# Attention's scalings on ScalarE, two row additions beside other stages, and each gather's first counts fetched one stage ahead

## The chip, the cores and the metric

The kernel runs on one core of a Trainium2 chip, in a single launch. The metric is the device time of one execution in microseconds (us). A core has a matrix engine (TensorE, in the rows PE; PEld is its loading of weights), a vector engine (VectorE, DVE), an activation engine (ScalarE, ACT), a general-purpose engine (GpSimd, POOL), and a queue that here only issues transfers (SyncE, SP). Each works through its own list of instructions in order; semaphores tie them together.

## The reference

Four layers, each a graph step and a feed-forward step, over 2500 nodes of 256 features and 80000 edges. Every step normalises x over its features, computes something and adds it to x:

```python
edge_index = jnp.stack([src, dst])
x = x + L0_gnn(layernorm(x))     # (mean over a node's edges) @ W_l.T + x @ W_r.T + b_r
x = x + L0_ffn(layernorm(x))     # two picked experts (gelu), then layer_norm(...) * gamma + beta
x = x + L1_gnn(layernorm(x))     # normalised sum over edges, @ W.T + b, layer norm, relu
x = x + L1_ffn(layernorm(x))     # 6 routed experts, 2 per node
x = x + L2_gnn(layernorm(x))     # gelu(agg @ W1 + b1) @ W2 + b2
x = x + L2_ffn(layernorm(x))     # 8 routed experts, 2 per node
x = x + L3_gnn(layernorm(x))     # attention of 4 heads over the edges, elu(out + b)
x = x + L3_ffn(layernorm(x))     # 8 experts, all weighted
```

In the attention, per head: e = exp(leaky_relu(el[src] + er[dst])), rowsum = segment_sum(e, src), and the output of a node is the sum over its edges of e / max(rowsum, 1e-12) times a row of x @ W, then elu(out + b).

## The kernel before

**Data.** The nodes are padded to 2560, 20 tiles of 128 (NT), 5 blocks of 512 (NB), 4 tiles to a block (TB). x stays in SBUF all the time as `m.x` (a tile's 128 nodes on the partitions, 256 features each). `m.xT` holds features on the partitions; `m.xn` and `m.o` are tiles of the size of x that the stages use in turn. The edges are turned once into a dense matrix of edge counts between nodes, in 16-bit floats, kept in device memory (`m.A_high`, transposed `m.AT_high`, and a low part that is only needed for large counts). A sum over edges is then a matrix product with the counts.

**Stages.** `program` (L2453) runs a list of phases. Each is a block with one list of instructions per engine; a new phase begins when all engines have ended the one before. In order, with the start in the profiled execution where the text needs it: setup and counts with a degree stage (`prepare`, L252, 360 us), gather g0 (380 us), experts e0 (526 us), norm n2 (664 us), norm n3 (696 us), gather g1 (709 us), routed experts e1, norm n6 (1085 us), gather g2 (1099 us), experts e2 (1200 us), the row addition b2 (1325 us), norm n8 (1334 us), routed experts e3 (1362 us), n9, attention (its main loop from 1716 to 2067 us), n10 (2068 us), experts e4 (2087 us to the end).

**A gather** (`phase_gather`, L772) multiplies the counts with y, 5 blocks of 512 result columns one after another. y is split into a high part (ScalarE, L936) and a low part (VectorE, L954), in 5 chunks of 4 tiles; TensorE waits for chunk after chunk in its first block. For each block TensorE runs 80 products of a 128 x 128 piece of y with 512 columns of counts (L877, the last two L895). A block's counts are 2,560 KB, in one of two buffers `at`. SP loads the first block's in five pieces when the phase begins (L835), each with its own semaphore, and every further block in one piece (L843), from the third on only when the block two before is through. Gather g0 writes its normalised rows to `m.o`, g1 to `m.xn`; both write `m.xT` behind a block's product, as g2 does.

**A norm** (`phase_norm`, L655): VectorE takes statistics of 20 tiles (L696), seven small steps on 20 columns (L241 to L247), a copy (L700), ScalarE the root, VectorE the reciprocal, then the rows are scaled, by ScalarE where there is a gamma (L745). n2 finishes layer 0's experts: gamma times the row, plus beta, plus x. There GpSimd adds beta to x by itself, block by block (L735), once both rows are loaded (L683, L684), while VectorE takes statistics of another tile; VectorE then multiplies by gamma (L718), waits for the block's beta (`shifted`) and adds to x (L721). n6 precedes g2 and n3 precedes g1.

**The experts** (`phase_experts`, L1580): TensorE computes a block's hidden values (`layer0`, L1743) one block ahead of the second product (`last`, L1771). ScalarE applies gelu twice (L1861, L1862), VectorE takes the low part (L2024) and adds results to the destination (L2047). Weights are split likewise: high part by ScalarE (L1868), low part by GpSimd (L1688, `low_weights`), which otherwise has nothing to do in this phase. In e0 the destination is `m.o` and x isn't touched; in e2 it is x.

**b2** (`phase_add_row`, L2065) loads one row to all partitions and adds it to all of x on VectorE.

**The attention loop** (`phase_attention`, L2082): 10 iterations, 2 pairs of heads times 5 blocks. In each, VectorE makes 40 masked count tiles (`mask`, L2318), ScalarE 20 plain ones (L2398), and TensorE multiplies them with the weighted features (L2426), masked ones for two heads (u = 1, 2) and plain ones for both (u = 0). ScalarE evicts each sum from PSUM (`evict`, L2386). The finishing of an iteration runs one iteration later in VectorE's list, as single steps put between pairs of masks by a generator:

```python
if (u - 1) * NT + t >= 8 and t % 2:
    next(steps, None)
```

Its steps: add two halves (L2329), scale by a factor per node and head (`s_g`, L2331), subtract and add four others (L2333 to L2339), four small ones for 1/rowsum (L2342 to L2348), scale by it (L2350), add the bias (L2354); then ScalarE takes an exponential (`exps`, L2390), and VectorE adds to x in two steps (L2360, L2362). In ScalarE's list `evict(it - 1, 2)` comes after five plain tiles of an iteration, and `evict(it, 0)`, `exps(it - 1)` and `evict(it, 1)` after its twenty.

## Time and profile before

| | |
|---|---|
| runs | 2480.57, 2481.78, 2483.63 us; median 2481.78 |
| profiled execution | 2481.93 us, its span 2480.2 us |
| busy share of the span | TensorE 78%, VectorE 61%, ScalarE 46%, GpSimd 15% |
| mean granted clock of TensorE | 0.89 of full speed |
| transfers | 222.59 MB, 90 GB/s on average |

The times are of the whole kernel; the shares are averages over stages that have different limits, so a change in one stage is read from that stage. The granted clock has two levels here, 1.00 (2.4 GHz) and 0.50 (1.2 GHz); values between are means over a stretch. In the rows, a tile's name leaves out its number (`g_at` is the gather's `at`), and two instructions of one engine may overlap by some 0.1 us, so what an instruction costs in a series is the time from one start to the next.

### The profile page before, as it was taken

The page shows a single profiled execution, that of the slowest core. Times are in us where ns is not written, and L with a number is a line of the kernel's source. Part 1 is how long each engine was busy: PE and PEld are TensorE (multiplying, and loading weights), DVE is VectorE, ACT ScalarE, POOL GpSimd, SP SyncE. Part 2 cuts the span into 40 slices and gives each one's busy share as a digit, 9 for nine tenths or more (in the row PEclk, how much of TensorE's full clock was granted, in tenths as well). Part 3 has the DMA queues.
Part 4 walks back from the last instruction along what each step waited for, and adds up shares of the span by engine and source line. Part 5 has one row for each costly group of instructions (what it writes and reads, how often), then busy time and mean ns, then how long its engine had stood idle before and what let it go on. Part 6 is the DMA issues. An engine that isn't in the chain of part 4 may idle for free. (4 is left out here: it accounts for less than half of the span.)

```text
span 2480.2 us, 38997 instructions
## 1 busy us (share of the span) xinstructions
PE 1941.6 (78%) x12631; PEld 1564.9 (63%) x12632; DVE 1519.1 (61%) x2808; ACT 1130.5 (46%) x2105; POOL 367.5 (15%) x319
## 2 busy tenths in 40 slices
PE   4888888949649659829795499644999995999997
PEld 2455554539625348704594499624988884788886
DVE  7997772454555356650335555377999995555554
ACT  0468882125221148610443277423443442566674
POOL 1000000000100037700000477422000000001010
PEclk9999999969869869959897599866999996899999
DMA  1235554210033136543101355321333220000001
GB/s 52 95 139 210 209 208 153 78 35 1 5 124 113 36 109 194 154 167 128 35 1 49 124 168 170 109 75 52 96 103 101 75 73 28 2 26 13 26 13 42
DMA packets 135056, 222.59 MB, mean 90 GB/s; under 512 B 18237, under 2 KB 100669, under 8 KB 134771
## 3 DMA queue, kind: packets, MB, share of 16 engines
q1 hardware_dynamic: 124775, 192.62, 23.0%
q0 software_dynamic: 10128, 27.93, 3.6%
q8 instruction: 96, 1.57, 0.3%
q14 instruction: 57, 0.47, 0.1%
HBM read 146.26 MB, written 74.24 MB: 89 GB/s over the span
## 5 line engine op out<-in xcount | busy, mean ns | idle before, releaser
L877 PE MATMUL g_ps<-g_at,g_y 128*128 128x512 f16 x1170 | 261.7, 384 | 125.5 <-DMA g_at<-counts_t_high 119.9
L2024 DVE TENSOR_TENSOR e_h_low<-x_feat,e_h_high 128x512 fp32r<-128x512 f32 (+1 forms) x240 | 169.5, 709 | 233.7 <-ACT e_h_high L1862 233.7
L877 PEld LDWEIGHTS g_ps<-g_at,g_y 128*128 128x128 f16 x1170 | 115.3, 99 | 266.6 <-DMA g_at<-counts_t_high 121.1
L2318 DVE SCALAR_TENSOR_TENSOR att_masked<-dinv_row,att_thr,x_feat 128x512 fp32r<-128x512 f32 x400 | 276.8, 747 | 9.2 <-PEq L2150 3.0
L1861 ACT ACTIVATE x_feat<-e_hps,e_b 128x512 f32<-128x512 f32 (+1 forms) x240 | 177.7, 741 | 209.8 <-issue 99.6
L2426 PE MATMUL att_ps<-att_xl_parts,att_masked 128*128 128x260 f32 x1600 | 244.3, 291 | 22.3 <-DVE att_masked L2318 20.9
L2426 PEld LDWEIGHTS att_ps<-att_xl_parts,att_masked 128*128 128x128 f32 x1600 | 211.0, 189 | 40.6 <-DVE att_masked L2318 32.4
L478 DVE TENSOR_TENSOR hot_key<-o_tok,dinv_row x240 | 195.7, 816 | 0.0
L526 PE MATMUL count_ps<-hot_key,hot_lo 128*128 x960 | 178.6, 311 | 18.4 <-DVE hot_key L478 14.5
L1771 PE MATMUL e_yps<-e_w_high,e_h_high 128*128 128x256 f32 (+1 forms) x640 | 183.0, 286 | 2.2 <-DVE e_h_low L2024 2.2
L1771 PE MATMUL e_yps<-e_w_high,e_h_low 128*128 128x256 f32 (+1 forms) x640 | 181.7, 284 | 0.0
L1771 PE MATMUL e_yps<-e_w_low,e_h_high 128*128 128x256 f32 (+1 forms) x640 | 181.6, 284 | 0.0
L1862 ACT ACTIVATE e_h_high<-e_hps,e_b 128x512 fp32r<-128x512 f32 (+1 forms) x240 | 176.6, 736 | 0.0
L2398 ACT ACTIVATE att_plain<-x_feat 128x512 fp32r<-128x512 f16 x200 | 117.8, 627 | 78.4 <-PE att_ps L2426 73.8
L2426 PE MATMUL att_ps<-att_xl_parts,att_plain 128*128 128x260 f32 x800 | 125.4, 288 | 30.0 <-ACT att_plain L2398 30.0
L526 PEld LDWEIGHTS count_ps<-hot_key,hot_lo 128*128 x960 | 95.1, 99 | 80.2 <-issue 42.7
L1743 PE MATMUL e_hps<-e_x_high,e_w_high 128*128 128x512 f32 (+1 forms) x320 | 126.7, 396 | 21.1 <-POOL e_w_low L1688 20.0
L1413 POOL DMA_INDIRECT e_x_rows<-xn_rows,e_get_i x104 | 126.5, 1216 | 59.1 <-issue 29.6
L581 ACT ACTIVATE turn_high<-count_ps 128x320 f16<-128x320 f32 x160 | 74.6, 466 | 119.6 <-PE count_ps L534 90.3
L478 DVE TENSOR_TENSOR hot_lo<-o_tok,dinv_row 128x512 f16 x240 | 100.3, 418 | 46.0 <-PE count_ps L526 38.4
L2426 PEld LDWEIGHTS att_ps<-att_xl_parts,att_plain 128*128 128x128 f32 x800 | 109.3, 192 | 30.1 <-ACT att_plain L2398 30.1
L1688 POOL TENSOR_TENSOR e_w_low<-a3xn_tok,e_w_high 128x512 fp32r<-128x512 f32 x23 | 29.1, 1295 | 660.6 <-ACT e_w_high L1868 660.6
(481 smaller groups left out, 4725.5 us busy)
## 6 DMA issues: line engine op xcount, KB each, us to landing
g_at<-counts_t_high SPq DMA_DIRECT2D x12, 2560.0 KB
x_feat<-counts_high SPq DMA_DIRECT2D x40, 640.0 KB, 4.1
e_w_in<-in_L_ffn_W SPq DMA_DIRECT2D x35, 512.0 KB, 3.8
e_w_in<-in_L_ffn_expert_w SPq DMA_DIRECT2D x56, 256.0 KB, 3.8
counts_t_high<-turn_high SPq DMA_DIRECT2D x20, 640.0 KB, 4.6
counts_t_low<-turn_low SPq DMA_DIRECT2D x20, 640.0 KB, 5.9
counts_high<-count_row SPq DMA_DIRECT2D x20, 640.0 KB, 2.9
counts_low<-count_row SPq DMA_DIRECT2D x20, 640.0 KB, 4.1
```

The costliest lines, as they stand in the source:

```text
L478: return dve.tensor_tensor(out.rearrange("p u (w d) -> p u w d", d=2), numbers.rearrange("p (w d) -> p w d", d=2).unsqueeze(1).to_broadcas ...
L526: mm = pe.matmul(acc[:, q % 4, 0:KW], hot_lo[:, j, ds(slot, P)], hot_key[:, j, ds(slot, KW)], start=False, stop=False, skip_group_check=True)
L877: pe.matmul(ps[:, k, :], y2[:, part, s, k * P:(k + 1) * P], at[:, b % 2, :, s, :], start=(s == 0 and part == 0), stop=False, skip_group_ch ...
L1413: pool.indirect_dma_start(x_rows[:, b % XB, q, :], None, m.xn_rows[:, :], bass.IndirectOffsetOnAxis(ap=r.get_i[:, b * RT + q:b * RT + q + ...
L1743: mm = pe.matmul(h_ps[0][:, f, 0:width(b)], w_parts[0][w][:, u, k, f * P:(f + 1) * P], x_parts[x][:, k, b * BLK:b * BLK + width(b)], start ...
L1771: mm = pe.matmul(y_ps[0:tokens, q, 0:D], h_parts[-1][h][:, v % 2, k, q * P:q * P + tokens], w_parts[-1][w][:, u, k, :], start=(k == 0 and ...
L1861: act.activation(h_sb[i][:, f, 0:w], h_ps[i][:, f, 0:w], func, bias=bias, scale=scale)
L1862: act.activation(h_parts[i][0][:, v % 2, f, 0:w], h_ps[i][:, f, 0:w], func, bias=bias, scale=scale).then_inc(h_act[i], 1)
L2024: dve.tensor_tensor(h_parts[i][1][:, v % 2, f, 0:w], h_sb[i][:, f, 0:w], h_parts[i][0][:, v % 2, f, 0:w].bitcast(F32), ALU.subtract).then_ ...
L2318: dve.scalar_tensor_tensor(S[:, n % RING, :], EL[:, it % 2, u - 1, :], thr[:, t, h:h + 1], A[:, t, :], ALU.is_gt, ALU.mult).then_inc(maske ...
L2398: act.activation(plain[:, n % ARING, :], A[:, t, :], ACT.Copy).then_inc(plain_a, 1)
L2426: mm = pe.matmul(ps[:, n % 2 * TB + q, 0:PW], side[:, q * P:(q + 1) * P], moving, start=(t == 0), stop=(t == NT - 1))
```

## The change

- Attention: the two wide scalings leave VectorE. The scaling by `s_g` is done by ScalarE in the eviction of u = 1 and 2: instead of one instruction over four tiles, four of 130 columns with a scale pointer and one for the other columns of all four. The scaling by 1/rowsum becomes eight instructions of 64 columns ahead of the exponential in `exps`. VectorE signals that 1/rowsum is made, leaves one step empty, and waits for the eight before it adds the bias.
- `phase_add_row` is gone. Its row is loaded at the start of g2 (ahead of the counts) and added to x by GpSimd, block by block, in g2.
- Beta leaves n2. Its row is loaded in e0 behind the first weights and added to x by GpSimd in e0, block by block, behind the low weights of the second expert.
- A gather's first block of counts gets a place of its own and is loaded in an earlier stage, as one transfer of 2,560 KB: for g0 in `prepare`, into `m.o`, when the counts are stored; for g1 in n2 and for g2 in n6, into `m.xT`. SP waits for it at that stage's end. The five pieces and their semaphores go, and the third block is loaded without waiting, because the first no longer uses a buffer of `at`.

```diff
 prepare, sync
             sp.sem_inc(written, 1)
+            tile, src = ahead
+            sp.dma_start(tile, src).then_inc(ahead_in, 16)
             sp.wait_ge(kept, 1)
...
             sp.wait_ge(stored, 16)
+            sp.wait_ge(ahead_in, 16)
 phase_norm, sync
+            if ahead is not None:
+                for tile, src in ahead:
+                    sp.dma_start(tile, src).then_inc(ahead_in, 16)
+                sp.wait_ge(ahead_in, 16 * len(ahead))
 phase_norm, vector
-                    if shift_x:
-                        dve.wait_ge(shifted, b + 1)
+                    if finish == "add":
                         dve.tensor_tensor(xv, v, xv, ALU.add).then_inc(ready, TB)
 phase_norm, gpsimd
-            if shift_x:
-                pool.wait_ge(affine_in, 32)
-                for b in range(NB):
-                    xv = part(m.x, b)
-                    pool.tensor_tensor(xv, xv, gb[:, 1:2, :].to_broadcast([P, TB, D]), ALU.add).then_inc(shifted, 1)
 phase_gather, sync
-            for c in range(NB):
-                cut = slice(c * TB, (c + 1) * TB)
-                sp.dma_start(at[:, 0, :, cut, :], m.AT_high[0:TB, :, c * BLK:(c + 1) * BLK].rearrange(
-                    "t p (s n) -> p t s n", n=P)).then_inc(first_in[c], 16)
+            if row is not None:
+                sp.dma_start(bias_sb[:, :], row.partition_broadcast(P)).then_inc(bias_in, 16)
...
-                if b >= 2:
+                if b >= 3:
                     sp.wait_ge(agg_mm, b - 1)
 phase_gather, tensor
+            def columns(b, s):
+                return at[:, b % 2, :, s, :] if b else first[:, :, s, :]
...
-                        pe.wait_ge(first_in[s // TB], 16)
                         pe.wait_ge(y_low, s // TB + 1)
 phase_gather, gpsimd
+            if row is not None:
+                pool.wait_ge(bias_in, 16)
+                for b in range(NB):
+                    xv = part(m.x, b)
+                    pool.tensor_tensor(xv, xv, bias_sb[:, :].unsqueeze(1).to_broadcast([P, TB, D]), ALU.add)
 phase_experts, sync
             load_pair(sp, 0)
+            if row is not None:
+                sp.dma_start(row_sb[:, :], row.partition_broadcast(P)).then_inc(row_in, 16)
 phase_experts, gpsimd
             low_weights(pool, 0, 1, 0)
+            if row is not None:
+                pool.wait_ge(row_in, 16)
+                for b in range(NB):
+                    xv = m.x[:, b * TB:(b + 1) * TB, :]
+                    pool.tensor_tensor(xv, xv, row_sb[:, :].unsqueeze(1).to_broadcast([P, TB, D]), ALU.add)
 phase_attention, finish (vector)
-                    own.join(dve.tensor_tensor(ov, ov, sg.unsqueeze(3).to_broadcast([P, TB, GRP, DA]), ALU.mult))
-                    yield
...
-                    own.join(dve.tensor_tensor(rs[:, 1, :, :], rs[:, 1, :, :], sf, ALU.mult))
+                    dve.tensor_tensor(rs[:, 1, :, :], rs[:, 1, :, :], sf, ALU.mult).then_inc(rs_made, 1)
                     yield
-                    own.join(dve.tensor_tensor(fin[:, :, :, :], o[:, :, :, 0:DO],
-                                               rs[:, 1, :, :].unsqueeze(3).to_broadcast([P, TB, GRP, DO]), ALU.mult))
                     yield
+                    dve.wait_ge(fin_scaled, (it + 1) * TB * GRP)
 phase_attention, evict and exps (scalar)
+                    for q in range(TB):
+                        t = it % NB * TB + q
+                        act.activation(sums[:, it % 2, q, u, 0:2 * DA], banks[:, q, 0:2 * DA], ACT.Copy,
+                                       scale=s_g[:, t, h:h + 1])
+                    act.activation(sums[:, it % 2, :, u, 2 * DA:PW], banks[:, :, 2 * DA:PW], ACT.Copy).then_inc(evicted, 1)
...
                 def exps(it):
+                    act.wait_ge(rs_made, it + 1)
+                    for q in range(TB):
+                        for u in range(GRP):
+                            act.activation(fin[:, q, u, :], o[:, q, u, 0:DO], ACT.Copy,
+                                           scale=rs[:, 1, q, u:u + 1]).then_inc(fin_scaled, 1)
                     act.wait_ge(fin_done, it + 1)
 program
+        first0 = first_view(m.o[:, :, :].rearrange("p t d -> p (t d)"))
+        first = first_view(m.xT[:, :, :].rearrange("p k n -> p (k n)"))
...
-            lambda: phase_add_row(nc, m, "b2", i["L2_gnn_b2"]),
```

## Rows read from the trace of the kernel before

**Rows 1.** Table by stretch, attention: start:end, length, busy time (count) per engine, clock, DMA.

```profile
1780.00:1812.00 32.00, 29.43 (x225) 27.57 (x224) 31.43 (x51) 15.05 (x24) 0.00 (x0) 1.00 0.28 85
```

**Rows 2.** Who waited for whom, attention loop: total us, times, longest.

```profile
ACT att_neg L2390 <- DVE att_fin L2354: 78.3, 9, 9.1
```

**Rows 3.** Order of time, VectorE in attention's second iteration: start, duration, instruction, count.

```profile
1751.01 0.69 DVE L2329 TENSOR_TENSOR att_o<-att_acc 128x520 f32<-128x520 f32 x1
1751.73 1.41 DVE L2318 SCALAR_TENSOR_TENSOR att_masked<-dinv_row,att_thr,x_feat 128x512 fp32r<-128x512 f32 x2
1753.06 0.69 DVE L2331 TENSOR_TENSOR att_o<-att_o,att_s_g 128x520 f32<-128x520 f32 x1
...
1768.09 0.16 DVE L2348 TENSOR_TENSOR att_rs<-att_rs,att_s_f 128x8 f32<-128x8 f32 x1
...
1769.62 0.68 DVE L2350 TENSOR_TENSOR att_fin<-att_o,att_rs 128x512 f32<-128x512 f32 x1
```

**Rows 4.** Order of time, norm n2.

```profile
667.26 11.53 POOL L735 TENSOR_TENSOR x_tok<-x_tok,n_gb 128x1024 f32<-128x1024 f32 x5 [85.82 <-DMA n_gb<-in_L_ffn_gamma]
670.47 1.47 DVE L241 TENSOR_TENSOR n_mean<-n_st 128x20 f32<-128x20 f32 x1
...
679.22 0.18 DVE L700 COPY n_var<-n_var 128x20 f32<-128x20 f32 x1
...
680.21 9.94 ACT L745 ACTIVATE o_tok<-o_tok,n_off,n_tmp 128x256 f32<-128x256 f32 x20 [0.56 <-DVE n_off L706]
```

**Rows 5.** Order of time, norm n3.

```profile
702.20 0.19 DVE L241 TENSOR_TENSOR n_mean<-n_st 128x20 f32<-128x20 f32 x1
...
703.21 0.18 DVE L700 COPY n_var<-n_var 128x20 f32<-128x20 f32 x1
```

**Rows 6.** Order of time, the starts of the gathers g0, g1 and g2.

```profile
381.33 5.77 DVE L954 SCALAR_TENSOR_TENSOR g_y<-xn_tok,g_y 128x1024 f16<-128x1024 f32 x5 [4.95 <-ACT g_y L936]
...
386.91 15.46 PE L877 MATMUL g_ps<-g_at,g_y 128*128 128x512 f16 x64 [10.64 <-DMA g_at<-counts_t_high]
...
710.29 5.77 DVE L954 SCALAR_TENSOR_TENSOR g_y<-xn_tok,g_y 128x1024 f16<-128x1024 f32 x5 [2.03 <-ACT g_y L936]
...
716.76 19.09 PE L877 MATMUL g_ps<-g_at,g_y 128*128 128x512 f16 x78 [54.39 <-DMA g_at<-counts_t_high]
...
1100.32 5.76 DVE L954 SCALAR_TENSOR_TENSOR g_y<-e1xn_tok,g_y 128x1024 f16<-128x1024 f32 x5 [2.03 <-ACT g_y L936]
...
1103.01 18.83 PE L877 MATMUL g_ps<-g_at,g_y 128*128 128x512 f16 x78 [54.82 <-DMA g_at<-counts_t_high]
```

**Rows 7.** Order of time, b2 and the start of n8.

```profile
1325.57 0.34 SPq L2072 DMA_DIRECT2D b_row<-in_L_gnn_b  x1
...
1334.62 0.34 SPq L683 DMA_DIRECT2D n_gb<-in_L_ffn_beta  x1
```

**Rows 8.** Table by stretch, the first five us of g1's first block.

```profile
716.00:721.00 5.00, 4.24 (x10) 1.49 (x11) 0.05 (x1) 0.00 (x0) 0.00 (x0) 0.50 1.09 387
```

**Rows 9.** Order of time, experts e0, VectorE and GpSimd.

```profile
570.71 0.69 DVE L2024 TENSOR_TENSOR e_h_low<-x_feat,e_h_high 128x512 fp32r<-128x512 f32 x1 [2.25 <-ACT e_h_high L1862]
...
576.68 4.76 POOL L1688 TENSOR_TENSOR e_w_low<-xn_tok,e_w_high 128x1024 fp32r<-128x1024 f32 x2 [28.17 <-ACT e_w_high L1868]
...
581.93 0.69 DVE L2024 TENSOR_TENSOR e_h_low<-x_feat,e_h_high 128x512 fp32r<-128x512 f32 x1 [2.25 <-ACT e_h_high L1862]
```

**Rows 10.** Waits of SP's queue, degree stage.

```profile
SPq L293 <- DMA counts_low<-count_row: 1.7, 1, 1.7
```

**Rows 11.** Order of time, degree stage, GpSimd.

```profile
370.08 1.20 POOL L314 DMA_INDIRECT spare_low<-counts_low,spare_at_i  x1 [8.91 <-DVE spare_at_i L400]
```

**Rows 12.** Order of time, ScalarE in attention's second and third iterations.

```profile
1764.92 1.04 ACT L2386 ACTIVATE att_acc<-att_ps 128x1040 f32<-128x1040 f32 x1 [3.17 <-PE att_ps L2426]
...
1781.96 3.22 ACT L2398 ACTIVATE att_plain<-x_feat 128x512 fp32r<-128x512 f16 x6
```

**Rows 13.** Order of time, ScalarE in e4, bias and scale by pointer.

```profile
2199.59 0.78 ACT L1861 ACTIVATE x_feat<-e_hps,e_b 128x512 f32<-128x512 f32 x1
```

More of the change, by code:

```diff
@@ L651, in phase_counts, with phase_norm @@
         all_stored += [(row_stored[u], NT // 2 * 32) for u in range(2)]
-        prepare(nc, m, mats, all_stored)
-def phase_norm(nc, m, name, src, out, outT=None, gamma=None, beta=None, scale=None, finish=None, kept=None, twice=False):
+        prepare(nc, m, mats, all_stored, m.first_block(m.o))
+def phase_norm(nc, m, name, src, out, outT=None, gamma=None, beta=None, scale=None, finish=None, kept=None, twice=False,
+               ahead=None):
     sem = nc.alloc_semaphore
@@ L712, in _ @@
             if gamma is not None:
-                dve.wait_ge(affine_in, 32)
+                dve.wait_ge(affine_in, 16 if beta is None else 32)
                 ga, be = (gb[:, i:i + 1, :].to_broadcast([P, TB, D]) for i in range(2))
@@ L767, in _, with phase_gather @@
                         mm.then_inc(turned, 1)
-def phase_gather(nc, m, name, y, kind, w=None, w_self=None, bias=None, gamma=None, beta=None, kept=None):
+def phase_gather(nc, m, name, y, kind, first, row=None, w=None, w_self=None, bias=None, gamma=None, beta=None, kept=None):
     sem = nc.alloc_semaphore
     at_in = [sem(f"{name}_at_in{i}") for i in range(2)]
-    first_in = [sem(f"{name}_first_in{c}") for c in range(NB)]
     agg_mm, agg_out, lin_mm, lin_out, bias_in, selfed, y_high, y_low, low_in, low_used = (
@@ L1648, in phase_experts @@
             wT = m.o[:, :, :].rearrange("p t d -> p (t d)")[0:EX, 0:NP].rearrange("p (t n) -> p t n", t=NT)
+        row_sb, row_in = sb("row", [P, D]) if row is not None else None, sem(f"{name}_row_in")
         def width(b):
@@ L2062, in _ @@
             pair(pairs - 1, False)
-def phase_add_row(nc, m, name, row):
-    sem = nc.alloc_semaphore
-    row_in = sem(f"{name}_in")
-    with nc.sbuf_tensor(f"{name}_row", [P, D], F32) as r, nc.Block() as block:
-        @block.sync
-        def _(sp):
-            sp.dma_start(r[:, :], row.partition_broadcast(P)).then_inc(row_in, 16)
-        @block.vector
-        def _(dve):
-            dve.wait_ge(row_in, 16)
-            dve.tensor_tensor(m.x[:, :, :], m.x[:, :, :], r[:, :].unsqueeze(1).to_broadcast([P, NT, D]), ALU.add)
 def phase_attention(nc, m, W, Wl, Wr, b):
```

48 lines of the change are left out of this document (30 added, 18 removed).

## The prediction

> **What bounds the kernel now.** I read the chain of waits first. It only shows the last stage, whose matmuls follow one another and which the change leaves alone, so I went stage by stage through the stretches that the change touches: a table by stretch, the list of who waited for whom, and the order of time. Four different limits came out.
>
> In the attention loop it is VectorE. In a stretch of 32 us, about one iteration, it is busy for 31.43 us, TensorE for 29.43 and ScalarE for 15.05 [rows 1]; ScalarE stands idle for 78.3 us over nine iterations at the exponential, waiting for VectorE [rows 2]. A mask pair takes 1.33 us of VectorE and each of the wide finishing steps between the pairs 0.72 (2.05 from one to the next) [rows 3].
>
> In the norm n2 it is a wait that no semaphore explains. Seven tiny statistics steps take from 670.47 to 679.22, 8.75 us [rows 4]; in n3 the same ones take from 702.20 to 703.21, 1.01 us [rows 5]. The only difference in that stretch is GpSimd adding beta: five adds in 11.53 us, 2.31 each, and one VectorE instruction gets through per add [rows 4].
>
> At the start of the three gathers it is a transfer. The first low parts of y are ready 1.22 us after L954's start, at 382.55, 711.51 and 1101.54 (5.77 us for five, so some 1.15 from one to the next), but the first matmul starts at 386.91, 716.76 and 1103.01 and waits for the counts [rows 6].
>
> Between e2 and n8 it is a stage of its own: b2's row load is issued at 1325.57 and n8's first load at 1334.62 [rows 7].
>
> **The change part by part.**
>
> *b2 goes.* Its whole stage is on the path: 1334.62 - 1325.57 = **9.05 us**. Its work, five adds on GpSimd, goes into g2. The row's load is ahead of g2's large loads in SP's queue, a small transfer. GpSimd starts when the row has landed. VectorE's L954 reads two SBUF tiles there, so it may alternate with the adds, as the tiny steps did in n2; each later low part could then be up to 2.31 us late. TensorE needs a new part only every 16 matmuls (ten in 4.24 us at the clock of a gather's start [rows 8], so some 6.8; at twice that clock 3.4, about the 2.31 + 1.15 of an add and a low part). I take nothing; the bounds are nothing and one add, 2.3 us, since a gain is excluded by the first part being made before.
>
> *n2 without beta on GpSimd.* The statistics should take what they take in n3: 8.75 - 1.01 = **7.74 us**. Behind them ScalarE's 20 scalings (9.94 us) and VectorE's adds stay as they are [rows 4]. The beta load leaves n2's queue, so gamma comes sooner; neither is waited for.
>
> *Beta beside e0.* GpSimd's queue has the adds behind its low weights of the second expert, which end at 576.68 + 4.76 = 581.44, and VectorE's first low part after that starts at 581.93; one round of the stage is 11.22 us (570.71 to 581.93) [rows 9]. The adds would run to some 593. By the n2 rows they may delay each of a round's four low parts (0.69 us each) by one add of 2.31: 4 x 2.31 = 9.2 us of delay in a round of which VectorE fills a third. The consumer, the second product, comes about one round later, and a block's hidden values are double-buffered. I take **nothing**, with 0 to 11.5 us (five adds, TensorE idle for all of it) as bounds. The row's load is queued behind the weights.
>
> The Trainium skill (SBUF — State Buffer, section "SBUF: two separate sides") speaks against this move: it says that GpSimd and a VectorE instruction with two SBUF inputs share a port pair that one of them holds for its whole instruction, while the other stands. This trace agrees, with 2.31 us per step in n2 [rows 4]; by that rule alone, without a round of slack, the sum would lose 11.5 us here.
>
> *The counts fetched one stage ahead.* For each gather 2,560 KB; at 387 GB/s, the rate of such loads at g1's start, that is 6.6 us [rows 8]. In n2 and n6 next to nothing else moves and both stages outlast it. SP waits for it at the end of the stage, so the cover is the rest of the stage; if that were gone, 6.6 us each. In the degree stage it is issued when the count stores have landed, after a wait of 1.7 us by SP [rows 10], some us before GpSimd's row fetch goes out at 370.08 [rows 11]. The end of that stage hangs on this fetch. I take nothing, with 0 to 6.6 us. SP's own store of the spare row waits behind the issue only, a fraction of a us. In the gathers the second and third blocks are then loaded at once, well ahead of use.
>
> Each gather's first matmul then follows the first low part: 386.91 - 382.55 = 4.36, 716.76 - 711.51 = 5.25, 1103.01 - 1101.54 = 1.47, minus 0.06 each for the hand-over: **10.9 us** [rows 6]. TensorE's clock is 0.50 (1.2 GHz) from 716 to 721, the first 5 us of work after idling through n2 and n3 [rows 8]. It starts as cold after the change, so this slow stretch moves along with the start. Whether it is shorter or longer is not to be read here: at most half of 5 us either way for a start.
>
> *Attention: what leaves VectorE.* L2331 and L2350, 0.72 us each, in nine iterations: 9 x 1.44 = **13.0 us**. TensorE doesn't take over: its 240 matmuls of an iteration need at most 240/225 x 29.43 = 31.4 us, VectorE's shortened iteration some 33 (20 pairs of 1.33, eight wide steps of 0.72, four small ones of 0.20) [rows 1, 3].
>
> *What ScalarE gets.* No row has a Copy with a scale pointer of this size, so I build it. A plain 512-element copy: 0.63 us, from one to the next (3.22 - 0.63)/5 = 0.52; the 1040-element eviction 1.04, so 0.78 ns an element and 0.12 us of fixed spacing; the activation with two pointers 0.78 instead of 0.63, so 0.075 a pointer [rows 12, 13]. A scaled one of 64 is then 0.12 + 0.05 + 0.075 = 0.245 us, eight with the last one's tail 2.07. An eviction becomes four of 130 (0.295 each) and one of 520: 1.82 instead of 1.04. The upper end is the dearest scaled row, 256 elements with two pointers, 9.94/20 = 0.50 us each [rows 4]; I take the low value, since cost follows the elements in the rows that I have.
>
> *The wait that this adds.* VectorE has two mask pairs between giving out the reciprocals and asking for the scaled rows. Counted from its first finishing step (1751.01), the reciprocals are out at 5 x 2.05 + 3 x 1.53 + 0.2 = 15.0 and asked for at 17.7: 2.7 us for 2.07 and 0.1 of hand-over [rows 3]. It fits. ScalarE arrives at this place in its queue behind the eviction at 1764.92 + 1.04, which is 14.95 after that step; with the longer eviction 15.7, so VectorE would wait 0.1 us there [rows 3, 12]. In most other iterations ScalarE has more in hand: it idled 8.7 us on average, 9.1 at most [rows 2]. Queued behind a longer wait would be all of VectorE's masks and through them TensorE. The longer eviction at an iteration's start delays TensorE by 0.78 us, within its slack.
>
> *The tail.* After the last mask nothing hides anything: eviction +0.78, L2331 -0.73, L2350 -0.73 and 2.17 for the scalings: +1.5 us. Attention: 13.0 - 1.5 - 0.1 = **11.4 us**.
>
> **Sum.** 9.05 + 7.74 + 10.9 + 11.4 = 39.1 us off the profiled execution's 2481.93 (span 2480.2): 2442.8. That execution is 0.15 us above the median of the runs, so **2442.7 us**.
>
> **Rivals.**
>
> *GpSimd's adds hold up e0.* For it: the n2 rows. Against: the round of slack. Five adds of 2.31 us: 2442.7 + 11.5 = 2454 us. Chance 0.08, for so far the trace shows the stall and not a case where it is hidden. This is what the port rule of the Trainium skill (SBUF — State Buffer, the same section) comes to if nothing takes up the delay.
>
> *Scalings too dear for two mask pairs.* At 0.50 us each, eight take 4.0; VectorE waits 1.4 us in each of nine iterations (12.5), and the tail is 2.7 longer: 2442.7 + 12.5 + 2.7 = 2458 us. For it: small instructions have a floor that I only extrapolate. Against: the two-pointer row costs just 0.15 more than the plain one. Chance 0.10.
>
> *The same mechanism on the other side, slower than before.* It decides when the wait per iteration eats 39.1/9 = 4.3 us: eight scalings in 2.7 + 4.3 - 0.1 = 6.9, 0.86 us each. At 0.9 us: 4.6 us in each of nine iterations and 5 in the tail, 2442.7 + 46 = 2489 us. Against it, the dearest scaled row is 0.50 us at four times the elements. Chance 0.03.
>
> *The early fetch lengthens the degree stage.* The spare row's fetch stands behind 2,560 KB: 6.6 us, 2449 us. For it: both go through the same DMA engines. Against: different queues, and the large one starts some us earlier. Chance 0.06.
>
> *The fetch doesn't do what it says:* the first matmul waits for something else, and the starts stay: 2442.7 + 10.9 = 2454 us. Against: both inputs of that matmul have a row [rows 6]. Chance 0.04.
>
> **The numbers.** My forecast has 0.69. The range reaches up to 2456, over both cases at 2454 and the one at 2449, and leaves out the two dear-scaling cases (0.13). Down it goes to 2438: attention's full 13.0 (1.6 more), and some 3 us from shorter slow stretches at the starts. 0.2%, 5 us, is about what a measurement of this kernel can tell from no change; every case but one is faster by more: 0.95, and 0.02 for the middle, 0.03 for slower.
>
> **What would show it.** In n2, the step from L241 to the copy before the root at about 1 us. No b2 stage. In each gather, the first matmul right behind the first low part. In attention, iterations some 1.4 us shorter, and next to no VectorE idle time released by ScalarE before the bias add. In e0, VectorE low parts of up to 3 us beside GpSimd's adds, and no TensorE idle time behind them. Wrong: VectorE waiting over 0.5 us an iteration for scaled rows; TensorE idle in e0 around 590; the degree stage ending later than 22 us after its start.

## The result, and the profile after

The changed kernel takes 2441.94 us (median of 4 runs, 2441.44 to 2442.75), the kernel before 2481.65 beside it (4 runs, 2480.57 to 2483.63): a ratio of 0.9837 with a 95% interval of 0.9821 to 0.9852 (the two medians alone give 0.9840). The prediction was 2442.7 in a range of 2438 to 2456. The profiled execution of the changed kernel took 2441.66 us, its span is 2440.0, 40.2 less than before. One of all the executions below, of experiment 7's kernel, took 5025.92 us at a mean granted clock of 1.00, for a reason that is not known, and is left out.

Where the 40.2 us come from is read from the transfers: in both kernels each stage but n3, n6, n9 and n10 begins with one that SP issues. The lengths from one such start to the next, in one profiled execution of each kernel:

| stage | before, us | after, us | difference | predicted |
|---|---|---|---|---|
| setup and counts | 360.07 | 360.27 | +0.20 | 0 |
| degree stage | 20.14 | 21.16 | +1.02 | 0 |
| g0 | 145.81 | 141.92 | -3.89 | -4.30 |
| e0 | 137.73 | 137.67 | -0.06 | 0 |
| n2 and n3 | 45.42 | 37.73 | -7.69 | -7.74 |
| g1 | 147.35 | 142.04 | -5.31 | -5.19 |
| e1 and n6 | 242.69 | 243.67 | +0.98 | 0 |
| g2 | 100.52 | 99.23 | -1.29 | -1.41 |
| e2 | 125.84 | 125.93 | +0.09 | 0 |
| b2 | 9.05 | gone | -9.05 | -9.05 |
| n8 | 27.53 | 27.18 | -0.35 | 0 |
| e3 and n9 | 284.93 | 284.39 | -0.54 | 0 |
| attention and n10 | 439.66 | 426.25 | -13.41 | -11.4 |
| e4 | 393.46 | 392.56 | -0.90 | 0 |

The four places named in the prediction give 9.05 + 7.69 + 10.49 + 13.41 = 40.6; the rest is the degree stage and stages whose work the change leaves alone (in n8 the two row loads change places).

**Norm n2**, VectorE in order of time in the changed kernel (start, duration, instruction, count). It answers to [rows 4]: the small steps take 1.02 us from L241 to the copy, as in n3 [rows 5].

```profile
667.74 0.19 DVE L241 TENSOR_TENSOR n_mean<-n_st 128x20 f32<-128x20 f32 x1
...
668.76 0.18 DVE L709 COPY n_var<-n_var 128x20 f32<-128x20 f32 x1
```

**The gathers' starts**, the same view, for g0, g1 and g2. They answer to [rows 6].

```profile
382.54 5.76 DVE L961 SCALAR_TENSOR_TENSOR g_y<-xn_tok,g_y 128x1024 f16<-128x1024 f32 x5 [4.98 <-ACT g_y L943]
...
383.82 17.41 PE L876 MATMUL g_ps<-o_tok,g_y 128*128 128x512 f16 x71 [6.37 <-DVE g_y L961]
...
699.86 5.77 DVE L961 SCALAR_TENSOR_TENSOR g_y<-xn_tok,g_y 128x1024 f16<-128x1024 f32 x5 [2.02 <-ACT g_y L943]
...
701.14 18.98 PE L876 MATMUL g_ps<-x_feat,g_y 128*128 128x512 f16 x78 [41.51 <-DVE g_y L961]
...
1085.58 12.23 DVE L961 SCALAR_TENSOR_TENSOR g_y<-e1xn_tok,g_y 128x1024 f16<-128x1024 f32 x5 [2.02 <-ACT g_y L943]
...
1086.86 18.98 PE L876 MATMUL g_ps<-x_feat,g_y 128*128 128x512 f16 x78 [53.22 <-DVE g_y L961]
1087.40 14.94 POOL L921 TENSOR_TENSOR x_tok<-x_tok,g_bias 128x1024 f32<-128x1024 f32 x5 [49.63 <-DMA g_bias<-in_L_gnn_b]
```

Each first product now waits for the low part (the name after the arrow) and starts 1.28 us after VectorE began it, where it waited for the counts before. In g2 GpSimd's additions stretch the five low parts from 5.76 to 12.23 us, and TensorE goes through its 78 products in 18.98 us all the same (18.83 before [rows 6], and 18.98 in g1, which has no additions).

**Experts e0**: first GpSimd's and VectorE's instructions in order of time, then a table by stretch (start:end, length, busy time (count) of PE, PEld, DVE, ACT and POOL, granted clock, DMA share, GB/s).

```profile
578.67 13.63 POOL L1739 TENSOR_TENSOR x_tok<-x_tok,e_row 128x1024 f32<-128x1024 f32 x5
...
579.19 10.85 DVE L2040 TENSOR_TENSOR e_h_low<-x_feat,e_h_high 128x512 fp32r<-128x512 f32 x4 [2.25 <-ACT e_h_high L1878]
589.96 1.65 DVE L2063 SCALAR_TENSOR_TENSOR o_tok<-e_yps,pair_w,o_tok 128x256 f32<-128x256 f32 x4
```

```profile
581.30:587.30 6.00, 6.00 (x50) 5.92 (x49) 6.00 (x4) 1.80 (x3) 6.00 (x3) 1.00 0.00 0
587.30:593.30 6.00, 6.00 (x35) 5.55 (x35) 6.00 (x8) 4.17 (x8) 5.00 (x2) 1.00 0.01 3
```

Four low parts of 0.69 us take 10.85, 2.7 each, the length of one addition (13.63 / 5); the last ends 6.1 us later after the stage's start than before (66.7 us for 60.6). TensorE is busy for 6.00 of 6.00 us beside it, and the stage is as long as before. So the stall that the Trainium skill (SBUF — State Buffer, section "SBUF: two separate sides") describes is there in full, and nothing on the path waits for it.

**The attention**: the table by stretch for one iteration, VectorE's and ScalarE's own waits (total us, times, longest), and both engines in order of time. The two SP rows are the same point of two iterations, seven apart.

```profile
1773.00:1806.00 33.00, 31.21 (x242) 29.51 (x241) 32.53 (x53) 18.28 (x40) 0.00 (x0) 1.00 0.31 97
```

```profile
ACT att_fin L2398 <- DVE att_rs L2346: 23.5, 9, 4.7
...
DVE att_fin L2351 <- ACT att_fin L2398: 2.1, 1, 2.1
```

```profile
1740.04 0.16 DVE L2346 TENSOR_TENSOR att_rs<-att_rs,att_s_f 128x8 f32<-128x8 f32 x1
1740.11 2.73 DVE L2318 SCALAR_TENSOR_TENSOR att_masked<-dinv_row,att_thr,x_feat 128x512 fp32r<-128x512 f32 x4
1742.77 0.68 DVE L2351 TENSOR_TENSOR att_fin<-att_fin,att_bias 128x512 f32<-128x512 f32 x1
...
1740.45 2.01 ACT L2398 ACTIVATE att_fin<-att_o,att_rs 128x64 f32<-128x64 f32 x8
...
1744.02 1.13 ACT L2390 ACTIVATE att_acc<-att_ps,att_s_g 128x130 f32<-128x130 f32 x4
1745.03 0.62 ACT L2392 ACTIVATE att_acc<-att_ps 128x520 f32<-128x520 f32 x1
...
1739.48 12.44 SPq L2146 DMA_DIRECT2D x_feat<-counts_high  x4
...
1970.95 12.44 SPq L2146 DMA_DIRECT2D x_feat<-counts_high  x4
```

In the kernel before, the mask behind the last small step ([rows 3] have the step, at 1768.09), and the same point of two iterations:

```profile
1768.28 1.42 DVE L2318 SCALAR_TENSOR_TENSOR att_masked<-dinv_row,att_thr,x_feat 128x512 fp32r<-128x512 f32 x2
```

```profile
1765.97 13.53 SPq L2146 DMA_DIRECT2D x_feat<-counts_high  x4
...
2008.49 13.52 SPq L2146 DMA_DIRECT2D x_feat<-counts_high  x4
```

An iteration takes (1970.95 - 1739.48) / 7 = 33.07 us, and took (2008.49 - 1765.97) / 7 = 34.65 before. VectorE is still the limit (32.53 busy of 33.00, TensorE 31.21), and it waits for scaled rows once, in the tail.

**The degree stage**, the stretch from 370 to 374, first in the kernel before, then in the changed one:

```profile
370.00:374.00 4.00, 3.55 (x13) 1.47 (x12) 3.11 (x15) 2.73 (x5) 1.20 (x1) 1.00 0.41 164
```

```profile
370.00:374.00 4.00, 3.66 (x10) 1.75 (x8) 2.12 (x11) 2.01 (x4) 1.15 (x1) 0.58 1.01 422
```

The early fetch moves 422 GB/s here, but what is slower is TensorE, whose granted clock is 0.58 on average instead of 1.00; its ten products for the degree row take 6.28 us instead of 5.21, and the stage's last steps hang on them.

### The profile page after: what moved, and what is told of

It reads as the page before. It is cut to its first block and busy times, and to the rows that moved or that the text cites. A ratio compares the mean times of both kernels' runs of the same rounds, so it can differ in the third digit from the quotient of the medians.

```text
span 2440.0 us, 39066 instructions
## 1 busy us (share of the span) xinstructions
PE 1935.5 (79%) x12631; PEld 1562.2 (64%) x12632; DVE 1506.2 (62%) x2787; ACT 1162.7 (48%) x2265; POOL 385.5 (16%) x324
## 5 line engine op out<-in xcount | busy, mean ns | idle before, releaser
L2040 DVE TENSOR_TENSOR e_h_low<-x_feat,e_h_high 128x512 fp32r<-128x512 f32 (+1 forms) x240 | 178.0, 746 | 228.6 <-ACT e_h_high L1878 228.6
L2437 PE MATMUL att_ps<-att_xl_parts,att_masked 128*128 128x260 f32 x1600 | 236.0, 288 | 15.1 <-DVE att_masked L2318 11.4
L876 PE MATMUL g_ps<-g_at,g_y 128*128 128x512 f16 x936 | 205.3, 379 | 5.6 <-DVE x_feat L999 5.6
L876 PEld LDWEIGHTS g_ps<-g_at,g_y 128*128 128x128 f16 x936 | 91.3, 98 | 114.4 <-issue 7.5
```

The lines of the kernel that those rows point to most:

```text
L876: pe.matmul(ps[:, k, :], y2[:, part, s, k * P:(k + 1) * P], columns(b, s), start=(s == 0 and part == 0), stop=False, skip_group_check=True)
L2040: dve.tensor_tensor(h_parts[i][1][:, v % 2, f, 0:w], h_sb[i][:, f, 0:w], h_parts[i][0][:, v % 2, f, 0:w].bitcast(F32), ALU.subtract).then_ ...
L2437: mm = pe.matmul(ps[:, n % 2 * TB + q, 0:PW], side[:, q * P:(q + 1) * P], moving, start=(t == 0), stop=(t == NT - 1))
```

## The experiments

All start from the changed kernel. They were measured later than the comparison above; beside them the kernel before took 2483.11 to 2485.15 us (medians), the changed kernel 2444.02 and 2445.82, ratios of 0.9838 and 0.9842. So times are compared by their ratio to the kernel before, and stage by stage. Stages that no experiment touches wander from execution to execution: e1 with n6 between 242.7 and 246.2 us, e3 with n9 between 284.3 and 286.3, e4 between 392.6 and 394.7. So do, where their work is the changed kernel's, g2 (98.9 to 100.0), e2 (124.3 to 126.2) and the attention with n10 (426.3 to 427.8).

### 1. The scalings on VectorE again

`phase_attention` of the kernel before, the rest as changed:

```diff
+own.join(dve.tensor_tensor(ov, ov, sg.unsqueeze(3)..., ALU.mult))
+own.join(dve.tensor_tensor(fin, o[..., 0:DO], rs[:, 1, :, :].unsqueeze(3)..., ALU.mult))
-act.activation(fin[:, q, u, :], o[:, q, u, 0:DO], ACT.Copy, scale=rs[:, 1, q, u:u + 1])
```

> Only the attention is as before: both scalings on VectorE, everything else as changed. Theory: the iteration goes from 33.07 us back to 34.64, nine times 1.57, and the tail gets 1.2 shorter, so 2441.9 + 14.1 - 1.2 = 2454.9 us. Of the 1.57, 1.44 are the two wide steps and 0.12 is VectorE's wait for its own last small step, which is not there when that step signals ScalarE instead. Rival: part of the attention's gain comes from elsewhere (an earlier start of the loop, another clock of TensorE); then the iteration stays under 34.4 us and the time under 2453. The degree stage and e1, each 1.0 us longer than before in the profile of the changed kernel, should be as long here as there if the change is the reason, and may be anything within 1 us if they wander from execution to execution.

Measured: 2458.27 us, ratio 0.9904 (0.9887 to 0.9920), 0.0067 or some 16 us above the changed kernel's; its attention with n10 took 440.05 us, 13.8 more than in the changed kernel, 0.4 more than before, and an iteration 34.65. All of the attention's gain sits in these steps. The whole kernel's 16 us are 3 more than the 13.0 expected, with some 4 us of uncertainty; two of its four executions took 2455.7 us and two 2461, and the profiled one is of the faster two. The degree stage took 20.62 us here and e1 245.36: both wander.

### 2. The first counts loaded in the gather, and 3. the rows behind them

First, SP issues five pieces into the same place when the gather begins; then, in the second kernel, the gather's small rows come behind the pieces in SP's queue instead of ahead of them:

```diff
+for c in range(NB):
+    sp.dma_start(first[:, :, cut, :], m.AT_high[0:TB, :, c * BLK:(c + 1) * BLK]...).then_inc(first_in[c], 16)
...
+pe.wait_ge(first_in[s // TB], 16)
 pe.wait_ge(y_low, s // TB + 1)
```

> Each gather loads its first counts itself again, in five pieces when it begins, into the place where the changed kernel keeps them. Theory: the first matmul starts 4.4, 5.2 and 1.5 us after the first low part again, and the three gathers get 3.9 + 5.3 + 1.3 = 10.5 us longer: 2452.4 us. If the early fetch is what made the degree stage 1.0 us longer (21.16 instead of 20.14), that comes back: 2451.4; if it is where TensorE's granted clock happened to rise and fall, the stage is not bound to be 20.1. Rival: the gathers' starts hang on the low parts of y alone, and the fetch ahead gains next to nothing: under 2445 us.

> The gathers load their first counts themselves again, as in the run with the fetch in the gather, but the rows (bias, gamma and beta, and in g2 the row that GpSimd adds) are queued behind the five pieces instead of ahead of them. In the kernel before, the first piece was there 3.8 us after its issue in g2, where no row was ahead of it, and 6.3 us in g0 and g1, where one and three were; in the run with the fetch in the gather, where g2 has a row ahead, 5.7. Theory: a row that is spread to all partitions holds back the transfer behind it by some 2 us; then the first matmul starts 3.8 us after the first issue in all three gathers, which gives back 2.1 + 1.0 + 1.9 of that run's 2456 (in g1 the issue of the rows' 1.3 us as well): 2449 to 2452 us. Rival: the 2 us belong to where the transfer comes from or to what ran before, and the first matmuls still start 5.7 to 6.3 us after the first issue: 2455 us.

Measured: 2456.22 us, ratio 0.9890 (0.9873 to 0.9906), with the rows ahead; 2447.63, ratio 0.9851 (0.9831 to 0.9871), with the rows behind. The start of g2 in the first and in the second, in order of time:

```profile
1093.02 4.56 SPq L834 DMA_DIRECT2D x_feat<-counts_t_high  x5
...
1098.75 19.05 PE L879 MATMUL g_ps<-x_feat,g_y 128*128 128x512 f16 x78 [57.10 <-DMA x_feat<-counts_t_high]
```

```profile
1085.33 2.73 SPq L827 DMA_DIRECT2D x_feat<-counts_t_high  x5
...
1089.25 18.54 PE L879 MATMUL g_ps<-x_feat,g_y 128*128 128x512 f16 x78 [54.92 <-DMA x_feat<-counts_t_high]
```

From the first issue to the first product it is 5.73 us with a row ahead and 3.92 without; 5.60 and 3.88 in g0, 6.30 and 4.19 in g1. With the row ahead SP also takes longer to issue the five pieces (4.56 us for 2.73). So the starts do hang on the counts, and a large part of that wait was the small rows ahead of them. The gathers of the first kernel are 3.44, 5.86 and 3.84 us longer than in the changed one, 13.1 in all where 10.5 was expected: g2 now has a row ahead of its pieces, which it had not before. The second kernel's are 2.36, 1.82 and 1.10 longer, 5.3 in all, and its 2447.63 us fits the 2447.2 that this gives; swapping the rows gave back 7.9 us, the sign and the place that the theory named and more than its 5.0 to 6.3. In these two kernels, without a fetch in it, the degree stage took 20.16 us.

### 4. Beta in n2 again

```diff
+pool.tensor_tensor(xv, xv, gb[:, 1:2, :].to_broadcast([P, TB, D]), ALU.add).then_inc(shifted, 1)
...
+dve.wait_ge(shifted, b + 1)
```

> Beta is added by GpSimd in n2 again, and not in e0. Theory: n2's small steps from L241 to the copy go from 1.02 us back to about 8.8, so 2441.9 + 7.7 = 2449.6 us, and e0 stays at 137.7 us, since its adds cost nothing. Rival: the adds cost something in e0 that its unchanged length hides; then e0 gets shorter here by that much, and the time lies below 2448. Second rival: n2's stall was the load of beta, which fetched gamma later, and not the adds; then VectorE is not held for 2.3 us per step beside them.

Measured: 2450.25 us, ratio 0.9867 (0.9850 to 0.9883); n2 with n3 took 47.16 us, 9.4 more than in the changed kernel, and e0 137.68. GpSimd and VectorE in n2, in order of time:

```profile
665.49 11.54 POOL L744 TENSOR_TENSOR x_tok<-x_tok,n_gb 128x1024 f32<-128x1024 f32 x5 [87.69 <-DMA n_gb<-in_L_ffn_beta]
666.84 1.04 DVE L241 TENSOR_TENSOR n_mean<-n_st 128x20 f32<-128x20 f32 x1
667.80 2.37 DVE L242 TENSOR_TENSOR n_tmp<-n_st 128x20 f32<-128x20 f32 x1
...
674.66 0.16 DVE L245 TENSOR_SCALAR n_var<-n_var 128x20 f32<-128x20 f32 x1
...
677.31 0.18 DVE L709 COPY n_var<-n_var 128x20 f32<-128x20 f32 x1
```

VectorE's steps of 0.2 us end where GpSimd's additions end (2.31 us each from 665.49), and the last of them run when the five are through at 677.03: the adds are the stall, and e0 is no shorter without them. Not only steps with two inputs in SBUF are held: L244, with one, ran for 2.25 us (0.18 in n3), while the statistics of 256 columns ahead of L241, with one too, took their 0.41 us beside an addition. The size was off, because n2 is held until the additions end, and they began 5.37 us after the stage here and 3.51 before: beta's row, now the second and with the 2,560 KB queued right behind it, was there 4.97 us after its issue (at 660.52), where the second row of before took 3.10.

### 5 and 6. ScalarE's scalings cut into two, and into four

```diff
-act.activation(fin[:, q, u, :], o[:, q, u, 0:DO], ACT.Copy, scale=...)
+for w in range(0, DO, DO // 2):    # DO // 4 in the second kernel
+    act.activation(fin[:, q, u, w:w + DO // 2], o[:, q, u, w:w + DO // 2], ACT.Copy, scale=...)
```

> Each of ScalarE's eight scalings of 1/rowsum is cut into two of 32 columns; the result is the same. VectorE asks for the scaled rows 2.73 us after it began the last of its small steps, and in the changed kernel they are there after 2.2, so 0.5 us of room is left. Theory (a fixed part of 0.12 + 0.075 us per instruction and 0.78 ns an element, as in the prediction): sixteen take 3.5 us, VectorE waits 1.0 us in each of nine iterations and the tail grows by 1.5: 2441.9 + 9 + 1.5 = 2452.4 us. Rival: a floor per instruction as high as what the 64 columns took (0.25): 3.95 us, 1.45 us of waiting, 2441.9 + 13 + 2 = 2457 us. Second rival: cost follows the elements, or other engines have room for the wait: 2442 us.

> Each scaling of 1/rowsum is cut into four of 16 columns, 32 instructions in all; the result is the same. With the fixed part that two sizes now show (2.02 us for eight of 64 columns, 3.51 for sixteen of 32: 0.18 to 0.2 us each, the elements nearly nothing), 32 take some 6.6 us, and VectorE, which has 2.73 us of other work, waits 4.0 us in each of nine iterations: 36 us, and 4.6 in the tail. Theory: 2441.9 + 41 = 2483 us, as slow as the kernel before: here lies the point from which the prediction's third rival would have decided. Rival: from some length on TensorE's slack (31.1 of 33.07 us per iteration) or a queue gives out earlier, and the wait costs more than its length: over 2490 us. Second rival: ScalarE's waits overlap and less of it is paid: under 2470 us.

Measured: 2451.73 us, ratio 0.9883 (0.9862 to 0.9904), and 2482.65, ratio 0.9994 (0.9984 to 1.0005). VectorE's wait for the scaled rows in the two (total us, times, longest), and the scaling's row by line and form (count, busy us, mean ns) in the changed kernel and in the two:

```profile
DVE att_fin L2351 <- ACT att_fin L2399: 12.1, 10, 3.6
```

```profile
DVE att_fin L2351 <- ACT att_fin L2399: 41.6, 10, 6.5
```

```profile
L2398 ACT ACTIVATE att_fin<-att_o,att_rs 128x64 f32<-128x64 f32 x80 | 20.2, 336 | 23.5 <-DVE att_rs L2346 23.5
```

```profile
L2399 ACT ACTIVATE att_fin<-att_o,att_rs 128x32 f32<-128x32 f32 x160 | 35.1, 309 | 22.4 <-DVE att_rs L2346 22.4
```

```profile
L2399 ACT ACTIVATE att_fin<-att_o,att_rs 128x16 f32<-128x16 f32 x320 | 64.6, 294 | 23.5 <-DVE att_rs L2346 23.5
```

A quarter of the columns takes 294 ns instead of 336: nearly all of it is fixed. From one start to the next it is (2.02 - 0.336) / 7 = 0.24, 0.21 and 0.20 us, so sixteen take 3.51 us and 32 take 6.47. VectorE waits 0.93 and 3.88 us in each iteration, an iteration grows to 34.08 and 37.03, and with the second all that the change gained is gone: the tipping point of the prediction's third rival, about where it was put (6.9 us for the scalings of an iteration). An iteration grows by the wait and 0.08 us: it is paid in full, and hardly more.

The Trainium skill (ScalarE: Activation LUTs, section "What ACT_TABLE_LOAD costs") gives about 280 ns + 0.833 ns per column for an instruction with one pointer operand: 333, 307 and 293 ns here, which these rows bear out; the four from PSUM with 130 columns take 367 where it gives 388.

### 7. Without the empty step

```diff
 dve.tensor_tensor(rs[:, 1, :, :], rs[:, 1, :, :], sf, ALU.mult).then_inc(rs_made, 1)
 yield
-yield
 dve.wait_ge(fin_scaled, (it + 1) * TB * GRP)
```

> The empty step between giving out 1/rowsum and asking for the scaled rows is gone, so VectorE asks one pair of masks (1.33 us) earlier. The scalings are done 2.2 us after VectorE's last small step, and it would then ask 1.4 us after it. Theory: VectorE waits 0.8 us in each of nine iterations, 7.5 us in all: 2449.4 us. Rival: it is not lost, because the iteration's later steps then also come a pair earlier and something else had been waiting on them: 2442 us.

Measured: 2449.01 us, the median of three executions (2448.61 to 2449.97), ratio 0.9858 (0.9838 to 0.9877). The wait for the scaled rows in this kernel:

```profile
DVE att_fin L2350 <- ACT att_fin L2397: 9.2, 10, 2.1
```

It is 0.77 us in each of nine iterations, and an iteration takes 33.92 us instead of 33.07. One pair of masks between giving out and asking is too little, two are enough.

### 8. Beta added three times over in e0

```diff
-for b in range(NB):
-    pool.tensor_tensor(xv, xv, row_sb..., ALU.add)
+for again in range(3):
+    if again:
+        pool.wait_ge(row_done, again * NB)
+    for b in range(NB):
+        pool.tensor_tensor(xv, xv, row_sb..., ALU.add).then_inc(row_done, 1)
```

> GpSimd adds beta three times over in e0, fifteen additions of 2.7 us instead of five, so x gets three times beta. Theory (each low part of VectorE is held by one addition, and the second product, which needs it a round later, has a whole round of slack): the first round's four low parts come 6.7 us late, as in the changed kernel, and cost nothing; in each further round beside the additions VectorE needs four low parts of 2.7 us and four additions to the destination of 0.4, 12.5 us, where a round lasts 11.2, so 1.3 us of delay is added per round, and two more rounds end 9.3 us late with 11.2 of slack: e0 stays within 1 us of 137.7. Rival: there is less slack than a round (one block's hidden values ahead, minus the low part's own place in the order), and TensorE waits from the second round on: e0 longer by 5 to 20 us.

Measured: 2443.94 us, ratio 0.9836 (0.9816 to 0.9856), the changed kernel's own; e0 took 137.95 us. GpSimd and VectorE in order of time, then two stretches of a round each:

```profile
579.47 41.50 POOL L1743 TENSOR_TENSOR x_tok<-x_tok,e_row 128x1024 f32<-128x1024 f32 x15
...
592.33 9.49 DVE L2044 TENSOR_TENSOR e_h_low<-x_feat,e_h_high 128x452 fp32r<-128x452 f32 x4
601.74 1.65 DVE L2067 SCALAR_TENSOR_TENSOR o_tok<-e_yps,pair_w,o_tok 128x256 f32<-128x256 f32 x4
603.31 9.75 DVE L2044 TENSOR_TENSOR e_h_low<-x_feat,e_h_high 128x512 fp32r<-128x512 f32 x4
```

```profile
594.40:605.60 11.20, 11.20 (x74) 10.24 (x73) 11.20 (x9) 4.91 (x9) 11.20 (x5) 1.00 0.00 0
605.60:616.80 11.20, 11.20 (x74) 10.24 (x74) 11.20 (x9) 5.10 (x9) 11.12 (x5) 1.00 0.01 1
```

41.5 us of additions stay hidden, with TensorE busy for all of 11.20 us a round. The lateness does not even add up, as the theory had it (and it began with 6.1 us, not 6.7): in the later rounds four low parts take 9.5 to 9.8 us and the additions to the destination 1.65, in all just the round's 11.2. The latter read PSUM and one SBUF tile and run at their usual 0.4 us beside GpSimd. No low part ended more than 6.6 us later than in the same place before, so how much of the round's 11.2 us could be used up is not shown.

### 9 to 12. TensorE at work ahead of the gathers, and the tail

Two kernels, each beside the changed kernel itself, to see whether the cold starts that the prediction left as they were can be had too:

```diff
 phase_gather, tensor
+for q in range(6):
+    pe.matmul(ps[:, 0, :], first[:, 0, q, :], columns(0, q), start=True, stop=True, ...)
 phase_norm (n3 and n6), tensor
+pe.wait_ge(ready, 1)
+for _ in range(18):    # 8 in the second kernel
+    pe.matmul(ps[:, 0, 0, :], m.ident[:, :], m.ident[:, :], start=True, stop=True)
 phase_attention, last iteration
+own.join(dve.tensor_tensor(fin, o[..., 0:DO], rs[:, 1, :, :].unsqueeze(3)..., ALU.mult))
```

> The changed kernel itself, unaltered, so that it stands on the same chip as the next one and as this chip's runs of the kernel before. Expected: 2442 to 2444 us, a ratio of 0.983 to 0.985 to the kernel before.

> The changed kernel with two things added that its trace points to; the result is the same. First, TensorE is kept at work ahead of the gathers: six products of the first counts with themselves at each gather's start, in the 2.4 us before the first low part is ready, and 18 small products in n3 and in n6 while their rows are scaled; their sums are thrown away. In the changed kernel the granted clock is 0.50 in the first 3.6 to 4.0 us of each gather's products, and half of that, some 1.9 us, is lost. Second, in the last iteration of the attention, which nothing hides, VectorE scales by 1/rowsum itself (0.73 us for ScalarE's 2.04). Theory (the clock rises some 4 us after TensorE begins to work, whatever it works on, and holds over a gap of a us or two): g1 and g2 begin at full clock and gain 1.9 us each, g0, with 2.4 us of work ahead, 1.2; the tail gains 1.3; 2441.9 - 6.3 = 2435.6 us. Rival: the clock falls in the gap between the stages, or the added products delay the first real one (six take 2.6 us at half clock): the gathers gain nothing or lose 0.2 each, and only the tail's 1.3 is left, 2440.6 us or the changed kernel's own time.

> The changed kernel itself once more, beside the next one. Expected: 2442 to 2445 us, a ratio of 0.983 to 0.985.

> As the run with the added products, but 8 of them in n3 and in n6 instead of 18: the 18 took 7.2 us at half clock, 0.40 each, and made n3 3.5 us longer and n6 some 3, which ate what the gathers gained (1.6 in g0, 1.9 in g1, 2.0 to 2.5 in g2). Eight take 3.2 us, about as long as the rows' scaling, so n3 and n6 should be as long as in the changed kernel. Theory: what was gained stays, 1.6 + 1.9 + 2 + the tail's 1.3: 6 to 7 us under the changed kernel in the same job, a ratio to the kernel before lower by 0.0025. Rival: with 3.2 us of work, a gap and the six products at the gather's start the clock has not risen yet when the first real product starts, and g1 and g2 gain 1.2 to 1.6 each, as g0 does: 5.5 us under the changed kernel.

Measured: 2444.56 us (ratio 0.9842, 0.9828 to 0.9857) with 18 products, beside 2444.02 (0.9838, 0.9825 to 0.9851) for the changed kernel: nothing. With 8, 2441.22 (0.9829, 0.9816 to 0.9843) beside 2445.82 (0.9842, 0.9828 to 0.9856). TensorE in order of time, in the kernel with 18, then in the one with 8 with its stretch behind the first product of g1, then the same stretch of the changed kernel:

```profile
692.87 7.23 PE L771 MATMUL n_ps<-ident 128*128 128x128 f32 x36 [34.70 <-DVE xn_tok L719]
```

```profile
690.87 3.79 PE L771 MATMUL n_ps<-ident 128*128 128x128 f32 x16 [34.72 <-DVE xn_tok L719]
695.41 1.46 PE L868 MATMUL g_ps<-x_feat 128*128 128x512 f16 x6 [0.75 <-PEq L2588]
697.75 12.48 PE L882 MATMUL g_ps<-x_feat,g_y 128*128 128x512 f16 x57 [0.89 <-DVE g_y L967]
```

```profile
698.00:699.00 1.00, 1.00 (x6) 0.47 (x5) 1.00 (x2) 1.00 (x2) 0.00 (x0) 1.00 0.37 89
```

```profile
702.00:703.00 1.00, 1.00 (x4) 0.42 (x3) 1.00 (x2) 1.00 (x2) 0.00 (x0) 0.50 0.24 45
```

The 18 took 7.23 us, n3 grew by 3.5, and that ate much of what the gathers gained. The tail, from its eviction to the last addition to x, took 9.83 us instead of 11.16 in the kernel with 18, the 1.3 that the theory had. With 8, g1 starts at the full clock (six products in the microsecond behind its first, instead of four) and takes 140.06 us instead of 141.98, and g2 98.03 instead of 99.65, though the clock rose there only 1.25 us behind its first product; g0, where the clock rose only 5.6 us after the added products began, 141.70 instead of 141.93. By the medians this version is 4.6 us faster than the changed kernel, about what can be told apart, and the intervals overlap: the gathers' gain is shown in the trace, the whole kernel's is likely and no more. The theory's premise, a rise some 4 us after TensorE begins to work, did not hold: it came after 2.8 to 6.2 us of work, and with 8 products in n6 not in that work at all.

## Why the prediction was right, and where its terms were off

The time, the sign and the mechanism of each part came out as forecast. That the total came within 0.8 us (2442.7 and 2441.9) is luck: the attention with n10 gave 2.0 us more than forecast, the degree stage and e1 with n6 took 1.0 more each, and n8, e3 and e4 came out 1.8 shorter by themselves.

- **b2** (9.05) and **n2** (7.74, measured 7.69): as predicted. Experiment 4 shows that GpSimd's additions were n2's stall.
- **The gathers' starts** (10.9, measured 10.5): as predicted for this change. What the prediction did not see is why the counts were late: experiments 2 and 3 show that 5.3 us of it needed the earlier fetch, and that the rest was the order of SP's queue, which by experiment 3 a swap of lines would have given.
- **e0** (0, bounds 0 to 11.5): right, and with far more room than argued. The first rival (0.08) is refuted: thrice the additions cost nothing either. The argument, a round of slack, held, as far as 6.6 us of it were used. VectorE fills 4.6 of a round's 11.2 us in the kernel before, more than the third that the prediction took; that the low parts and the additions to the destination just fill a round was luck of the sizes.
- **g2's additions** (0, bounds 0 to 2.3): at most 0.15 us in the first block's products, and none is shown, as g1's take as long without additions.
- **Attention** (11.4, measured 13.0 without n10 and the setup, which came out 0.3 and 0.1 shorter): here a term was too small. VectorE's part was priced at 1.44 us an iteration and is 1.58. Of the 0.14 more, 0.12 is a wait: the last small step had waited for itself to end (0.19 from its start at 1768.09 to the next mask at 1768.28, [rows 3] have its 0.16), and now that it signals ScalarE the next mask follows after 0.07. The tail's +1.5 was 1.2, mostly because the five pieces of an eviction take 1.63 us together and not 1.82. The 0.1 of waiting did not appear: in the iteration that the prediction looked at ScalarE came to the scalings 0.2 us late, which the room took up, and in the others it stood ready some 2.4 us before 1/rowsum was made. The price of the eight scalings was right: 2.07 predicted, 2.02 measured; their spacing 0.24 and 0.245.
- **The rivals of dear scalings** (0.10 and 0.03): refuted, and experiments 5 to 7 show that the mechanism they name is real: VectorE pays the wait in full. The room was 0.5 us an iteration.
- **The degree stage** (0, bounds 0 to 6.6, which at 387 GB/s should be 6.8 for 2,560 KB of 1,024 bytes): "wrong if it ends later than 22 us after its start"; it took 21.16. Three executions without the fetch took 20.14 to 20.16. The rival (0.06) names a delay that is there: from issue to landing, GpSimd's row took 4.4 to 4.8 us in these three and 5.4 to 6.2 in the eleven with the fetch, about 1 us longer and not 6.6. In four of the eleven TensorE's clock rose once and stayed up; there VectorE waits 0.14 to 0.49 us for the row, and the stage took 20.27 to 20.62, longer by about as much. In the other seven the clock rose early and fell again, the stage took 20.74 to 21.20, and VectorE comes so late behind TensorE's products that it doesn't wait for the row. In the changed kernel's profile the early rise at 363.8 came ahead of the fetch's issue at 364.71, and in six of the seven the clock was at 0.50 already 3 us before the stage began, where it was at 1.00 in all other executions, so that pattern did not begin with the fetch. Whether the fall has to do with the fetch stays open, as it was not seen in the three without.

## What to carry to other kernels

Before a transfer is moved a stage ahead, look at what stands ahead of it in its queue: one to three rows of 1 KB, each spread over all partitions, held back 512 KB by some 2 us. An engine that is stalled for microseconds costs nothing where its consumer comes a round later, and everything where the next step needs it at once: the same additions cost 7.7 us in the norm and nothing in the experts. When small work goes to another engine, price it by the instruction first (on ScalarE 0.20 to 0.24 us each from 16 to 64 columns), and give it as many steps of cover as its series is long; the wait behind that point is paid in full.

## What the runs showed of the hardware

- A small row and a large transfer in one queue slow each other: with rows ahead, the first 512 KB were there 5.6 to 6.3 us after their issue, without 3.9 to 4.2; a row with 2,560 KB right behind it landed after 4.97 us instead of 3.10.
- Beside GpSimd's additions, VectorE's instructions with two SBUF inputs end only where an addition ends (2.3 to 2.8 us for 0.2 to 0.7), and so did a `tensor_scalar` with one (L244 of n2, 2.25 us for 0.18). Those with one input in PSUM (0.4 us each, experiment 8) and the statistics with one SBUF input (0.41 us, experiment 4) run undisturbed.
- TensorE's granted clock rises from 0.50 to 1.00 at no fixed time after TensorE begins to work: 2.8 us (g0 with added products, the kernel with 18), 3.9 to 4.0 (the changed kernel's gathers), 3.7 (n3, the kernel with 8), 5.2 (n6, the kernel with 18), 5.6 (g0, the kernel with 8) and 6.2 (n3, the kernel with 18).
- A small row fetched by GpSimd while 2,560 KB arrive through SP's queue lands 5.4 to 6.2 us after its issue, and 4.4 to 4.8 without them.
- On VectorE, a step of 128 x 8 that the engine itself waits for costs 0.19 us to the next start, and one that it does not wait for 0.07.
